# Sort steps dealt into the first feed-forward part, the pivot search behind it in bfloat16 products, and key block gathers beside the first attention

## The chip, the cores and the metric

The program runs on one core of one Trainium2 chip. The metric is device microseconds from start to end of one launch. A core has five engines with an instruction stream each: PE (TensorE, matrix products), DVE (VectorE), ACT (ScalarE), POOL (GpSimd) and SP (SyncE), which only issues transfers here. They wait for one another by semaphores. On-chip memory has 128 partitions.

## The reference

A small language model tower over 64 sequences of 256 tokens (16,384 tokens of 64 numbers), every stage added to the running value `h`:

```
h = tok(x)                                  # embedding, two small products, layer norm
h = h + recurrence(norm(h))                 # delta-rule recurrence along each sequence
h = h + moe(norm(norm(h)))                  # 8 experts 64->128->64, gates of the top 2
h = h + window_attention(norm(h))           # windows of 64 tokens, 8 heads of 8
h = h + gat_moe(norm(h))                    # graph attention over 262,144 edges sets gates of 4 experts
```

The last stage is what needs the sort. For every token (node) it wants a softmax over the edges that end there:

```
a_src, a_dst = (g*att_src).sum(-1), (g*att_dst).sum(-1)     # g = norm(h) @ W_gat, 16 numbers per node
e   = leaky_relu(a_src[src] + a_dst[dst])
agg = segment_sum(g[src] * exp(e - segment_max(e, dst)) / denom, dst)
```

## The kernel before, in words

**Stages.** The 16,384 tokens are 128 tiles of 128 (`NT=128`), cut into two parts of 64 tiles (`PARTS`). Each part goes through the recurrence (8 iterations of 8 tiles, `it(i)`, two lanes side by side), the first feed-forward part (FFN: norm, norm again, gates, then 8 groups `k`, each of four quarters `q` for pairs of experts), window attention (16 iterations of 4 tiles) and the node stage of the graph attention (8 iterations), which writes 24 numbers per node into the `node_table` in DRAM. Part 1 starts when part 0 has ended.

**Edges.** Beside part 0 DVE sorts the 262,144 edges by destination. A key holds destination and source; 128 rows hold 2048 keys each in two buffers `K[0]`, `K[1]`. The sort is a bitonic network of 192 steps (`network()`): exchanges ("x": a minimum and a maximum over all keys, lines L1037 and L1038, or L1042 and L1043 for the first ones), "sign" (L1058) and 14 "move" steps. In a move DVE only raises `s_sd` (L1061); SP stores the block to DRAM and loads it back with rows and columns exchanged (L281, L283), and the next exchange waits for that. A 193rd step reads the 32 pivots of each row (L1065) and lets SP store the sorted keys (L285 on).

**Where the sort steps stand.** DVE's program is written out in one order. `burst(i,t,most)` places up to `most` steps at six places of a recurrence iteration, where a clock of the planner (105 us per iteration, 2.5 us per step, 22 us per move) says that the data is back. What is left after the eighth iteration follows in one piece (`while at[0]<SORT`).

**Search.** For each of 32,768 node boundaries the kernel looks for the position in the sorted keys. *Pivots*: 32 chunks; DVE writes a 0/1 matrix `stp` (L1163, two buffers), PE multiplies it by the pivots' steps `dpv` (8 products of 128x128 by 128x32, float32), and DVE counts (`pivots_counted`, L1152 to L1154). The result `idx2` (L1168) frees POOL, which gathers 256 times 128 blocks of 64 keys (L420), 32 gathers in each of 8 rounds, into two landing buffers. *Rounds*: DVE compares a landed round with the thresholds (`search_round`, L1047 on); round r's gathers wait until round r-2 is used. In the kernel before the pivots stand between the recurrence and the FFN, and the rounds at fixed places: one before the gates, one behind them, one in front of each FFN group from k=3 on, one behind the FFN. `keys_apart` (L1185) splits the keys into source and destination and stands between the FFN's first two norms.

**POOL behind it.** When part 0's rows of the node table are stored (`s_tst`, L425), POOL gathers the table's rows for the early edges (960 gathers, L433), scatters the nodes' own terms (256, L442; the second half waits for part 1's node stage), gathers the rows of the late edges (1088, L450) and last the sums at the ends of the segments (256, L460). DVE works on what lands.

All products go through the one helper on L464 (`mm`), so a tile's name and shape tell them apart. L1289 is the FFN's multiplication by the gates, L1294 its sum, L1275 the addition to `h_res`; L1320 to L1332 are attention; L1174 to L1179 the norm.

## Time and profile before

| | |
|---|---|
| median of 3 runs | 5481.16 us (5477.91 to 5487.49) |
| the profiled execution, its own time | 5501.64 us |
| its span (first to last instruction) | 5499.9 us |
| busy: PE / DVE / ACT / POOL | 2728.7 / 2414.3 / 1248.0 / 2915.7 us |
| mean granted TensorE clock | 0.678 of 2.4 GHz |
| packets | 345,120, of which 214,943 under 512 bytes |

The page gives 1.7 us between the span and the profiled execution's own time. The profiled execution took 20.5 us more than the median; durations come from it. No engine is busy more than 53% of the span, so shares of busy time don't tell what bounds the kernel; the chain of waits and the order of the stages do. The granted clock of TensorE has two levels, 1.2 and 2.4 GHz; a clock of 0.50 in a stretch is the lower level throughout, 1.00 the upper.

### The profile page before, as it was taken

The page shows a single profiled execution, that of the slowest core. Times are in us where ns is not written, and L with a number is a line of the kernel's source. Part 1 is how long each engine was busy: PE and PEld are TensorE (multiplying, and loading weights), DVE is VectorE, ACT ScalarE, POOL GpSimd, SP SyncE. Part 2 cuts the span into 40 slices and gives each one's busy share as a digit, 9 for nine tenths or more (in the row PEclk, how much of TensorE's full clock was granted, in tenths as well). Part 3 has the DMA queues.
Part 4 walks back from the last instruction along what each step waited for, and adds up shares of the span by engine and source line. Part 5 has one row for each costly group of instructions (what it writes and reads, how often), then busy time and mean ns, then how long its engine had stood idle before and what let it go on. Part 6 is the DMA issues. An engine that isn't in the chain of part 4 may idle for free.

```text
span 5499.9 us, 73623 instructions
## 1 busy us (share of the span) xinstructions
PE 2728.7 (50%) x28112; PEld 2055.3 (37%) x29104; DVE 2414.3 (44%) x5221; ACT 1248.0 (23%) x2738; POOL 2915.7 (53%) x2870
## 2 busy tenths in 40 slices
PE   4667676258468767777587872022423324241000
PEld 3555565253157656565434662011212212121000
DVE  8855556555366523333446760023232323232234
ACT  2223222014244433333344540000110101010000
POOL 0000000037710077777767777777777777776774
PEclk8788877558679788888798985555555555555555
DMA  2024332305200091111162111021212222121113
GB/s 71 5 40 51 47 41 36 55 10 119 55 3 0 19 22 27 25 27 30 16 124 35 21 21 32 3 66 42 57 45 53 57 42 62 36 51 43 40 40 81
DMA packets 345120, 226.72 MB, mean 41 GB/s; under 512 B 214943, under 2 KB 302848, under 8 KB 342336
## 3 DMA queue, kind: packets, MB, share of 16 engines
q1 hardware_dynamic: 247472, 164.51, 15.2%
q0 software_dynamic: 92464, 49.28, 7.3%
q10 hardware_dynamic: 4896, 8.92, 0.7%
q8 instruction: 203, 3.33, 0.3%
q14 instruction: 85, 0.70, 0.0%
HBM read 136.08 MB, written 86.40 MB: 40 GB/s over the span
## 4 chain that ended last, share of the span: by engine, by line
POOL 52%; issue 18%; DVE 13%; PE 12%; DMA 3%; ACT 2%; POOLq 0%; SPq 0%; DVEq 0%; ACTq 0%
POOL arena L450 21%; POOL arena L433 17%; PE bank L464 12%; POOL arena L460 5%; POOL edge_dst_terms L442 4%; POOL arena L420 4%; DVE arena L1038 2%; DVE arena L1037 2%; DVE arena L1043 1%; DMA early_rows<-arena 1%; DVE arena L1042 1%; DVE arena L1320 1%; DVE arena L1325 1%; DMA arena<-sort_exchange 1%; DMA xT_d<-arena 0%
## 5 line engine op out<-in xcount | busy, mean ns | idle before, releaser
L464 PE MATMUL bank<-arena 64*64 64x64 f32 (+11 forms) x25478 | 2322.0, 296 | 1852.0 <-ACT arena L938 1200.1
L464 PEld LDWEIGHTS bank<-arena 64*64 64x64 f32 (+5 forms) x25478 | 1578.7, 166 | 1908.1 <-issue 1625.8
L450 POOL DMA_INDIRECT arena<-node_table,arena x1088 | 1157.4, 1064 | 331.6 <-issue 331.6
L433 POOL DMA_INDIRECT arena<-node_table,arena x960 | 939.3, 978 | 347.4 <-issue 288.3
L413 POOL IOTA arena<- 128x1024 int32 x1 | 1.0, 988 | 940.6 <-DVE h_res L1131 940.6
L420 POOL DMA_INDIRECT arena<-sorted_keys,key_block_idx x256 | 277.0, 1082 | 304.8 <-DVE key_block_idx L1168 227.1
L464 PE MATMUL bank<-ident,arena 128*128 128x128 f32 (+2 forms) x2048 | 304.8, 325 | 227.3 <-ACT arena L908 80.3
L464 PEld LDWEIGHTS bank<-ident,arena 128*128 128x128 f32 (+2 forms) x2048 | 273.4, 196 | 261.4 <-DVE arena L1326 106.6
L1380 DVE COPY arena<-arena 128x4 f32<-128x4 f32 x32 | 5.9, 184 | 807.2 <-DMA arena<-node_table,arena 806.7
L940 ACT ACTIVATE arena<-arena 128x512 f32<-128x512 f32 x32 | 20.1, 629 | 1408.0 <-DVE arena L1388 1408.0
L183 PEld LDWEIGHTS <-zero_b 128*128 128x128 bf16 x992 | 97.7, 99 | 581.3 <-DVE arena L1103 118.7
L460 POOL DMA_INDIRECT arena<-sums_sorted,arena x256 | 261.7, 1022 | 79.1 <-issue 77.7
L442 POOL DMA_INDIRECT edge_dst_terms<-arena x256 | 258.9, 1011 | 83.5 <-issue 83.5
L425 POOL TENSOR_TENSOR pool_spare<-pool_spare 1x1 f32<-1x1 f32 x2 | 0.6, 286 | 401.6 <-DMA node_table<-arena 401.6
L893 ACT ACTIVATE arena<-bank,arena 128x512 f32<-128x512 f32 x256 | 161.9, 684 | 225.7 <-PE bank L464 224.8
L1395 DVE TENSOR_TENSOR_SCAN arena<-arena 128x64 f32<-128x64 f32 x640 | 186.4, 372 | 1.1
L464 PE MATMUL bank<-pivot_steps,arena 128*128 128x32 f32 x512 | 109.4, 401 | 116.9 <-DVE arena L1163 116.9
L1037 DVE TENSOR_TENSOR arena<-arena 128x1024 f32<-128x1024 f32 x116 | 141.9, 1224 | 39.1 <-DMA arena<-sort_exchange 36.0
L1289 DVE SCALAR_TENSOR_TENSOR arena<-bank,arena 128x512 f32<-128x512 f32 x128 | 89.8, 746 | 154.9 <-PE bank L464 109.1
L464 PEld LDWEIGHTS bank<-pivot_steps,arena 128*128 128x128 f32 x512 | 109.3, 333 | 117.1 <-issue 117.1
L1364 DVE TENSOR_TENSOR arena<-bank,arena 128x512 f32<-128x512 f32 x64 | 44.3, 692 | 223.1 <-PE bank L464 223.1
L1038 DVE TENSOR_TENSOR arena<-arena 128x1024 f32<-128x1024 f32 x116 | 141.4, 1219 | 0.0
(377 smaller groups left out, 3046.4 us busy)
## 6 DMA issues: line engine op xcount, KB each, us to landing
arena<-expert_gates SPq DMA_DIRECT2D x64, 512.0 KB, 7.4
arena<-node_table,arena POOLq DMA_INDIRECT x2048
sums_sorted<-arena SPq DMA_DIRECT2D x32, 768.0 KB, 3.3
expert_out<-arena SPq DMA_DIRECT2D x64, 256.0 KB, 2.6
arena<-expert_out SPq DMA_DIRECT2D x16, 1024.0 KB, 5.8
sort_exchange<-arena SPq DMA_DIRECT2D x14, 1024.0 KB, 3.9
early_rows<-arena POOLq DMA_DIRECT2D x15, 768.0 KB, 3.6
arena<-early_rows SPq DMA_DIRECT2D x15, 768.0 KB, 4.3
```

Source lines behind the costliest of these rows:

```text
L183: if me=="pe": nc.tensor.ldweights(zero_b[:,:],tile_position=(0,0))
L420: G.indirect_dma_start(out=rows[:,u,:],out_offset=None,in_=keysb,in_offset=bass.IndirectOffsetOnAxis(ap=idx2[:,t:t+1],axis=0)).then_inc(s_ ...
L433: G.indirect_dma_start(out=early_b[j%2][:,c,:],out_offset=None,in_=tbl, in_offset=bass.IndirectOffsetOnAxis(ap=gidx[:,j*CW+c:j*CW+c+1],axi ...
L442: G.indirect_dma_start(out=ad_e,out_offset=bass.IndirectOffsetOnAxis(ap=sidx[:,h*NT+t:h*NT+t+1],axis=0), in_=nodeG[:,t,20:24],in_offset=No ...
L450: G.indirect_dma_start(out=rch[:,j%NB,c,:],out_offset=None,in_=tbl, in_offset=bass.IndirectOffsetOnAxis(ap=gidx[:,CA+j*CW+c:CA+j*CW+c+1],a ...
L460: G.indirect_dma_start(out=at[:,t,:],out_offset=None,in_=sums_d,in_offset=bass.IndirectOffsetOnAxis(ap=eidx[:,h*NT+t:h*NT+t+1],axis=0)).th ...
L464: mm=lambda o,a,b,st=True,sp_=True: nc.tensor.matmul(o,a,b,start=st,stop=sp_,skip_group_check=True)
L893: A.activation(B.hT[:,n%2,:],B.ps[n%2][:,:],ACT.Gelu,bias=fb1[:,n%8:n%8+1]).then_inc(B.ge,1)
L1037: V.tensor_tensor(y[:,:,0,:],x[:,:,0,:],x[:,:,1,:],ALU.min)
L1038: lk(V.tensor_tensor(y[:,:,1,:],x[:,:,0,:],x[:,:,1,:],ALU.max))
L1289: V.scalar_tensor_tensor(out=B.tm[:,q%2,:] if q else B.acc[:,k%2,:],in0=B.ps[2+m%2][:,:],scalar=fb2[l][:,q:q+1],in1=B.G[:,k%2,q,:],op0=ALU ...
L1395: last=V.tensor_tensor_scan(R[:,:,f],xe[:,0,:,head(f)],R[:,:,f],cin[:,f:f+1],ALU.mult,ALU.add)
```

## The change

1. **Sort plan.** A function `sort_plan()` makes, before the program is built, lists of how many steps stand at each place: seven places in a recurrence iteration (`PLACES`, with 9, 2, 5, 3, 4, 1 and 1 as the most), two before the gates of the first FFN part (`PRE_AT`), and one behind each of the 32 quarters of it (`FFN_AT`, two at most). What is left (`LEFT`) stands behind the FFN. SP's moves are dealt in the same way.
2. **Pivots.** They stand behind the FFN of part 0 instead of in front of it, and the steps `dpv` are split into a high and a low part in bfloat16; `stp` is bfloat16 too. Each float32 product becomes two bfloat16 ones.
3. **Rounds.** `keys_apart` stands behind the norm that precedes attention; rounds stand in front of attention's iterations 4, 6, 9, 11, 13 and 15, and the last two behind attention.

How many steps stand at each place (x exchange, s sign, M move; a slash between places):

| recurrence iteration | before (6 places) | after (7 places) |
|---|---|---|
| 0 and 1 | 12/3/5/4/5/3 | 9/2/5/3/4/1/1 |
| 2 | 4/0/2/0/5/3 | 9/2/5/2/0/1/1 |
| 3 | 5/0/3/0/0/3 | 0/2/5/3/3/0/1 |
| 4 | 10/0/0/4/0/3 | 2/2/5/3/3/0/1 |
| 5 | 10/0/0/4/1/3 | 3/0/5/3/4/1/0 |
| 6 | 10/0/0/4/2/0 | 0/2/3/0/0/1/1 |
| 7 | 12/1/0/4/3/0 | 9/2/0/0/4/1/1 |
| sum | 160 | 140 |

Then before: 33 steps in one piece. After: xxx before the gates; in the FFN's groups (four quarters each) xx/xx/xx/xx, sM/-/-/xx, xx/xx/M/-, -/xx/xx/xx, xx/xx/xs/M, -/-/xx/xx, xx/xM/-/-, xx/xx/xx/xx; behind it xxxM.

```diff
+PLACES=((2.0,9),(29.0,2),(40.0,5),(53.0,3),(64.0,4),(80.0,1),(92.0,1))
+BEFORE_FFN=2
+def sort_plan():
+    net=[kind for kind,d,up in network()]+["move"]
+    at=0; ready=0.0
+    def take(now,most):
+        nonlocal at,ready
+        n=m=0
+        while n<most and at<len(net) and now>=ready:
+            now+=2.4; n+=1
+            if net[at]=="move": ready=now+20.0; m+=1
+            at+=1
+        return n,m
+    rec=[[take(i*100.0+t,most) for t,most in PLACES] for i in range(ITA)]
+    t=ITA*100.0+10.0
+    pre=[take(t+30.0*k,3) for k in range(BEFORE_FFN)]
+    t+=30.0*BEFORE_FFN
+    ffn=[[take(t+36.0*k+9.0*q,2) for q in range(4)] for k in range(ITA)]
+    left=len(net)-at
+    return rec,pre,ffn,left
...
-        axs=bump(AX0,W0); stp=[axs([1024]),axs([1024])]; iov=axs([1024],I32); cnt=axs([16,31])
+        axs=bump(AX0,W0); stp=[axs([1024],BF16),axs([1024],BF16)]; iov=axs([1024],I32); cnt=axs([16,31])
...
                         for h,s in HALVES:
                             sp.dma_start(B.G[s,k%2,:,:],gd[...]...).then_inc(B.gl[k%2],16)
+                    if part==0 and k: sort_moves(sum(m for _,m in FFN_AT[k-1]))
+                if part==0:
+                    sort_moves(2*XL+1-moved[0])
+                    sp.dma_start(keys2,K[0]).then_inc(s_ks,16)
+                    sp.dma_start(pvp[1:P,:],pv[0:P-1,:]).then_inc(s_ks,16)
...
                 for B in FL: pe.wait_ge(B.ha,k1); pe.wait_ge(B.ge,8*k1)
-                if part==0: pe.wait_ge(s_w2,16*8)
+                if part==0:
+                    for c in range(32):
+                        b=c//2
+                        pe.wait_ge(s_sp,c+1)
+                        if c%2==0 and b>=8: pe.wait_ge(s_sq,b-7)
+                        for u in range(8):
+                            k=8*(c%2)+u
+                            mm(PS[b%8][:,k*32:(k+1)*32],stp[c%2][:,u*P:(u+1)*P],dph[:,:],True,False)
+                            r=mm(PS[b%8][:,k*32:(k+1)*32],stp[c%2][:,u*P:(u+1)*P],dpl[:,:],False,True)
+                        r.then_inc(s_sm,1)
+                    pe.wait_ge(s_sq,16)
+                    pe.wait_ge(s_w2,16*8)
...
-                if run==0:
-                    while at[0]<SORT: sort_step()
...
                 norm(part,H,xn)
-                if part==0: keys_apart()
+                if part==0: steps_of(PRE_AT[0])
                 norm(part,xn,xn,s_xn)
-                if part==0: search_round()
+                if part==0: steps_of(PRE_AT[1])
...
-                if part==0: search_round()
...
-                    if part==0 and k>=3: search_round()
                     for q in range(4):
...
+                        if part==0: steps_of(FFN_AT[k][q])
                 for l in range(2): result(l,k1-1)
...
+                if part==0:
+                    steps_of((LEFT,0))
+                    pivots()
                 norm(part,H,xn)
-                if part==0: search_round()
+                if part==0: keys_apart()
...
-                    if part==0 and i==9 and used[0]<8: search_round()
+                    if part==0 and i in (4,6,9,11,13,15): search_round()
```

DVE, the end of part 0's recurrence (its last write to `h_res`) and what follows. Before:

```order
L1131 TENSOR_TENSOR h_res<-bank,arena 128x256 x2
L1037 TENSOR_TENSOR arena<-arena 128x1024
L1038 TENSOR_TENSOR arena<-arena 128x1024
L1037 TENSOR_TENSOR arena<-arena 128x2x512
L1038 TENSOR_TENSOR arena<-arena 128x2x512
```

and after, where L1157 is the same write and L1178 on the norm:

```order
L1157 TENSOR_TENSOR h_res<-bank,arena 128x256 x2
L1169 MEMSET eps 128x1
L1171 CAST iota8<-iota8_i 128x8
L1172 TENSOR_SCALAR iota_below_four<-iota8 128x4
L1264 MEMSET arena 128x1056
L1265 TENSOR_SCALAR arena<-iota8 128x8
L1178 TENSOR_REDUCE ln_stat<-h_res 128x32
```

The 33 sort steps and the pivot search no longer stand between the recurrence and the norm.

DVE, the first quarters of the FFN's group 0. Before (L1289 the gates' multiplication, L1294 the sum):

```order
L1289 SCALAR_TENSOR_TENSOR arena<-bank,arena 128x512 x4
L1294 TENSOR_TENSOR arena<-arena 128x512 x2
L1289 SCALAR_TENSOR_TENSOR arena<-bank,arena 128x512 x2
L1294 TENSOR_TENSOR arena<-arena 128x512 x2
L1289 SCALAR_TENSOR_TENSOR arena<-bank,arena 128x512 x2
L1294 TENSOR_TENSOR arena<-arena 128x512 x2
```

and after, where L1317 and L1322 are the same two and L1069, L1070 a sort exchange:

```order
L1317 SCALAR_TENSOR_TENSOR arena<-bank,arena 128x512 x2
L1069 TENSOR_TENSOR arena<-arena 128x8x128
L1070 TENSOR_TENSOR arena<-arena 128x8x128
L1069 TENSOR_TENSOR arena<-arena 128x16x64
L1070 TENSOR_TENSOR arena<-arena 128x16x64
L1317 SCALAR_TENSOR_TENSOR arena<-bank,arena 128x512 x2
L1322 TENSOR_TENSOR arena<-arena 128x512 x2
L1069 TENSOR_TENSOR arena<-arena 128x32x32
L1070 TENSOR_TENSOR arena<-arena 128x32x32
```

Two exchanges now stand between one quarter's work and the next.

SP, from the FFN's first gate loads (L334) on, after the change; L307 and L309 are a sort move's store and load:

```order
L334 DMA arena<-expert_gates 64x4x512 x12
L307 DMA sort_exchange<-arena 128x2048
L309 DMA arena<-sort_exchange 128x128x16
L334 DMA arena<-expert_gates 64x4x512 x4
L307 DMA sort_exchange<-arena 128x2048
L309 DMA arena<-sort_exchange 128x128x16
L334 DMA arena<-expert_gates 64x4x512 x8
```

Before, the 32 gate loads stood in one row with no move between them.

## Rows read from the trace of the kernel before

**Rows 1.** Page, part 4: the chain that ended last, shares of the span.

```profile
POOL 52%; issue 18%; DVE 13%; PE 12%; DMA 3%; ACT 2%; POOLq 0%; SPq 0%; DVEq 0%; ACTq 0%
POOL arena L450 21%; POOL arena L433 17%; PE bank L464 12%; POOL arena L460 5%; POOL edge_dst_terms L442 4%; POOL arena L420 4%; DVE arena L1038 2%; DVE arena L1037 2%; DVE arena L1043 1%; DMA early_rows<-arena 1%; DVE arena L1042 1%; DVE arena L1320 1%; DVE arena L1325 1%; DMA arena<-sort_exchange 1%; DMA xT_d<-arena 0%
```

**Rows 2.** POOL's waits: us in total, times, longest us.

```profile
POOL pool_spare L425 <- DMA node_table<-arena: 401.6, 2, 401.0
POOL arena L420 <- DVE key_block_idx L1168: 227.1, 1, 227.1
POOL edge_dst_terms L442 <- issue: 83.5, 256, 3.0
```

**Rows 3.** Stretches: length; busy us of PE, PEld, DVE, ACT, POOL; clock; DMA; GB/s.

```profile
36.00:948.00 912.00, 604.52 (x8896) 508.18 (x9392) 600.24 (x1069) 248.79 (x576) 0.00 (x0) 0.78 0.26 34
948.00:1055.00 107.00, 0.00 (x0) 0.00 (x0) 70.02 (x62) 0.00 (x0) 0.99 (x1) 0.51 0.33 39
1055.00:1176.00 121.00, 109.41 (x512) 109.30 (x512) 50.36 (x121) 0.00 (x0) 0.00 (x0) 0.50 0.09 29
1285.00:1508.00 223.00, 151.47 (x600) 51.22 (x600) 103.96 (x148) 73.44 (x116) 173.03 (x165) 0.80 0.46 94
1508.00:1845.00 337.00, 259.59 (x3072) 214.11 (x3072) 228.11 (x549) 153.34 (x458) 18.39 (x16) 0.86 0.01 2
```

**Rows 4.** DVE's timeline, one iteration of part 1's recurrence, which holds no sort step.

```profile
2128.75 0.48 DVE L1086 TENSOR_SCALAR arena<-arena 128x512 f32<-128x512 int32 x1
...
2145.55 0.43 DVE L1089 TENSOR_SCALAR arena<-arena 128x512 f32<-128x512 f32 x1 [15.13 <-ACT arena L825]
...
2155.16 0.83 DVE L1096 TENSOR_TENSOR arena<-arena 128x256 f32<-128x256 f32 x2 [3.16 <-ACT arena L834]
...
2168.89 0.69 DVE L1106 TENSOR_TENSOR arena<-bank,arena 128x512 f32<-128x512 f32 x1 [7.57 <-PE bank L464]
...
2192.62 0.69 DVE L1114 TENSOR_TENSOR arena<-bank,arena 128x512 f32<-128x512 f32 x1 [7.92 <-PE bank L464]
...
2220.87 0.48 DVE L1086 TENSOR_SCALAR arena<-arena 128x512 f32<-128x512 int32 x1
```

**Rows 5.** DVE's timeline, a sort move's return and the exchange behind it.

```profile
993.57 1.23 DVE L1037 TENSOR_TENSOR arena<-arena 128x1024 f32<-128x1024 f32 x1 [18.00 <-DMA arena<-sort_exchange]
...
995.97 1.22 DVE L1037 TENSOR_TENSOR arena<-arena 128x1024 f32<-128x1024 f32 x1
```

**Rows 6.** A bfloat16 weight load (zeros, in the recurrence): ns min/median/max.

```profile
L183 PEld LDWEIGHTS <-zero_b x992: 95/96/151, 36.9 to 2680.1; 128*128 128x128 bf16 x199
```

**Rows 7.** DVE's timeline, the pivot search; a chunk that waits, and a count.

```profile
1061.27 0.06 DVE L1156 MEMSET pivot_steps<- 128x1 f32 x1 [5.15 <-DMA pivot_nodes_row_above<-pivot_nodes]
...
1085.03 0.75 DVE L1163 TENSOR_SCALAR arena<-arena,shifted_firsts 128x1024 f32<-128x1024 int32 x1 [2.66 <-PE bank L464]
1085.70 0.67 DVE L1152 TENSOR_TENSOR arena<-bank,arena 128x496 f32<-128x496 f32 x1
...
1087.11 0.17 DVE L1154 SCALAR_TENSOR_TENSOR search_a<-bank,search_b 128x16 f32<-128x16 f32 x1
```

**Rows 8.** DVE's timeline, FFN of part 0: quarters, and a round that waits.

```profile
1309.46 1.41 DVE L1289 SCALAR_TENSOR_TENSOR arena<-bank,arena 128x512 f32<-128x512 f32 x2 [2.73 <-PE bank L464]
...
1323.80 1.41 DVE L1289 SCALAR_TENSOR_TENSOR arena<-bank,arena 128x512 f32<-128x512 f32 x2 [1.53 <-PE bank L464]
1327.94 1.41 DVE L1289 SCALAR_TENSOR_TENSOR arena<-bank,arena 128x512 f32<-128x512 f32 x2 [2.73 <-PE bank L464]
...
1441.92 2.29 DVE L1047 TENSOR_TENSOR arena<-arena,node_thresholds 128x2048 f32<-128x2048 f32 x1 [22.26 <-DMA arena<-sorted_keys,key_block_idx]
...
1447.06 2.73 DVE L1289 SCALAR_TENSOR_TENSOR arena<-bank,arena 128x512 f32<-128x512 f32 x4
```

**Rows 9.** DVE's timeline, the start of attention's second iteration.

```profile
1568.60 2.48 DVE L1320 TENSOR_TENSOR arena<-bank,arena 128x512 f32<-128x512 f32 x4 [1.89 <-ACT arena L906]
```

**Rows 10.** POOL alone in part 1's attention: length, POOL busy, clock, DMA share, GB/s.

```profile
2970.00:3200.00 230.00, 168.07 (x178) 0.95 0.13 20
```

More of the change, by code:

```diff
@@ L276, in _, with sort_moves @@
             sp.dma_start(tbl.rearrange("(p a b) f -> p a (b f)",p=P,a=8),zfill[:,0:384].unsqueeze(1).broadcast_to((P,8,384))).then_inc(s_zs,16)
[L277 to L279 removed]
+            moved=[0]
+            def sort_moves(count):
+                for _ in range(count):
+                    moved[0]+=1; n=moved[0]
                     sp.wait_ge(s_sd,n)
[L281 to L294 removed]
+                    if n<=2*XL:
+                        k=merge_at((n+1)//2,(n+1)%2)
+                        sp.dma_start(sort2,K[k]).then_inc(s_st,16)
+                        sp.wait_ge(s_st,16*n)
+                        sp.dma_start(K[1-k].rearrange("p (q l) -> p q l",l=16),sortx).then_inc(s_sl,16)
+            sort_moves(sum(m for row in REC_AT for _,m in row))
             for l in range(LANES):
@@ L309, in _ @@
                 k0,k1=t0//8,t1//8; b0,b1=k0//2,k1//2
+                if part==0: sort_moves(sum(m for _,m in PRE_AT))
                 sp.wait_ge(s_ws,b1)
@@ L1067, in sort_step, with steps_of, burst @@
                     V.tensor_copy(rowbase[:,:],rowp_f[:,:]).then_inc(s_sd,1)
-            SORT=len(NET)+1
-            clock=[0.0]
-            def burst(i,t,most):
-                now=i*ITER_US+t
-                while most and at[0]<SORT and now>=hold[0]:
-                    kind=NET[at[0]][0] if at[0]<len(NET) else "move" if at[0]==len(NET) else "x"
-                    sort_step(); most-=1; now+=2.5
-                    if kind=="move": hold[0]=now+ROUND_US
-            ITER_US=105.0; ROUND_US=22.0
+            def steps_of(place):
+                for _ in range(place[0]): sort_step()
             dve.wait_ge(s_key,1)
             def it(i):
+                def burst(k):
+                    if i<ITA: steps_of(REC_AT[i][k])
                 def step(fn,*need):
```

97 lines of the change are left out of this document (43 added, 54 removed).

## The prediction

> **What bounds the kernel now.** I read the chain of waits first: POOL holds 52% of it, and its gathers on L433, L450 and L460 with the scatters on L442 make 47% of the span [rows 1]. Then POOL's waits, to see what starts that work: it waited once for a long time, 401.0 us, for the last store of part 0's node table (L425), and behind that the longest wait of any scatter was 3.0 us [rows 2]. So from the moment at which part 0's table is stored (call it S, 1933 in the profiled execution's time) POOL runs without a pause, and part 1's compute is hidden beside it. What comes before S decides, microsecond for microsecond. Then the stretches [rows 3] tell what stands before S: the recurrence 912 us (36 to 948); 107 us in which PE and ACT do nothing and DVE finishes the sort; 121 us of pivot search; then the norms and gates (109 us to the FFN's first multiplication at 1285), the FFN with 223 us, norm and attention with 337, and the last 88 to S. Nothing in the change touches a later instruction. I therefore work out the shift of S and take it as the shift of the end.
>
> **The recurrence, from 912 to about 846.** An iteration without sort steps takes 92.1 us (2128.75 to 2220.87), and in it DVE waits 15.1 us behind the first place, 3.2 behind the second, 7.6 behind the third, 7.9 behind the fifth [rows 4]. An exchange takes 2.40 us, measured start to start [rows 5]. Steps are free up to the wait that follows them; the rest lengthens the iteration. Twelve steps at the first place cost 12 x 2.4 - 15.1 = 13.7, nine cost 6.5. At the second place three cost 4.0 and two 1.6; at the third five cost 12 - 9 = 3 in both kernels (the wait of 7.6 and some shorter ones behind it). For the fourth and fifth I take 2.9 and 5.7 us as covered, less than the longest single wait: four steps on the fourth cost 6.7, three 4.3; five on the fifth 6.3, four 3.9. Three on the old last place cost about 3.8, one on each of the two new ones nothing. With the numbers of steps in the table of the change this gives, iteration by iteration, 37.5, 37.5, 10.1, 3.8, 13.6, 16.0, 12.2, 20.4 before: 151 us over 8 x 92.1 = 737, together 888, where the trace has 912. The missing 24 us I can't place. After: 19.3, 19.3, 11.1, 8.9, 8.9, 10.1, 1.6, 10.4, together 90, so 827 without the missing part and 841 to 851 with it. I take 846: -66 us (bounds: -56, all of the 24 stays and places three to five hide less; -80).
>
> **The sort's tail and the pivots in front of the norm: -107 and -121** [rows 3]. Both go. The norms start at once. SP's loads of the FFN's weights, which lay beside the pivots, now lie beside the two norms; they are needed only at the first turned tile. Between the gates and the first multiplication one search round goes that was hidden in a wait for the gate loads; in front of the gates go one round (5.1, as 1441.92 to 1447.06 in [rows 8]) and the splitting of the keys (2.6), and three exchanges come (7.2). Together 0.
>
> **The FFN, from 223 to about 238: +15.** Before, a group of four quarters takes 18.5 us (1309.46 to 1327.94), a quarter 4.14, and three rounds then make DVE wait some 21 us each for POOL's gathers (22.26 in the row shown) [rows 8]; DVE is busy 104 of 223 us [rows 3]. Those waits go. The steps come: 40 exchanges of 2.4 and 2 signs of 1.3 make 99 us. DVE's own work is 104 less five rounds of 5.1 = 78, so DVE alone has 177. A quarter with two exchanges takes 2.6 + 4.8 = 7.4 on DVE, more than PE's 4.14, and PE works one quarter ahead, in the other bank: I count it as hidden. Eleven quarters have no exchange and are bound by PE: some 1.5 us each, 16. The start with its wait for the gate loads: 5. And the four moves: a landing takes 18.0 us [rows 5] when the DMA engines are free; here the gate loads share them (share 0.46 on the mean, with half of the time empty [rows 3]), so I take 18 to 26. Between a move and the next exchange the plan leaves two to four quarters, worth some 8 to 14 us at PE's pace where the plan's own clock counts 9 each, so each move makes DVE wait 5 to 15 us: four times 10 is 40. The sum is 238. Bounds: 210 (landings hidden) and 290 (below).
>
> **The pivots behind the FFN: +73.** The last four steps (7.4), the wait for the rows stored by SP (5.2, as [rows 7]), the split of the steps and the 32 shifts (3.6), the chunks, and 1 us for the index. A chunk has 16 products as before, when 512 took 109.4 us at the lower clock, 1.2 GHz (0.50 throughout) [rows 3]: 3.42 us per chunk, 0.214 per product, and DVE waited 2.66 us in each [rows 7]. A bfloat16 load of 128 columns takes 96 ns in the median, alone [rows 6]. The trace has no bfloat16 product of this shape. Bounds: PE as slow as now, 109 us; PE no longer the bound, DVE's own work of 0.67 per chunk and 1.5 per two chunks [rows 7], 1.42 x 32 = 46 us. The nearest row is the load: 16 x 0.107 (half of 0.214, a little above 96 ns) = 1.7 us, 55 us in all. I take 56.
> The Trainium skill (TensorE: Matmul & The Clock Gate, Weight-path perf modes) says that weights of 128 columns that aren't float32 load by a faster path, measured at about twice the speed. By that, PE falls below DVE's pace, the chunks take 46 us, and the total is 10 us less. The row of zero weights shows 96 ns, which doesn't look like the fast path, so I stay with 56.
>
> **Attention, from 337 to 398: +61.** From the index (T) on POOL gathers eight rounds. In the FFN's stretch POOL issued 165 gathers in 223 us, 1.35 us each [rows 3], so 43.3 us per round; beside part 1's attention 178 in 230 us, 1.29 each [rows 10]: attention doesn't slow them. Norm (26.5), splitting the keys (2.6), constants and the first products (8): attention starts at T+37 and takes 18.7 us per iteration (1545 to 1845, 16 of them). A round costs DVE 5.1 us, of which the 1.9 us wait at an iteration's start hides a part [rows 9]: 3.3 to 5.1 each. Round 0 is used at iteration 4 (T+112 to 117), so round 2's gathers can't start before T+117 and land at T+162; from there they follow each other at 43 us, held up once for 12 by round 2's use at iteration 9: round 6 at T+348, round 7 at T+392. Attention ends at T+356. DVE then waits some 30 us for round 7, uses it (5.1), and starts the next norm at T+398. Before it started 337 us after the FFN. The last 88 us to S are unchanged. Bounds: +45 (gathers at 1.29), +80.
> The Trainium skill (SBUF — State Buffer, Who interferes with whom) warns that GpSimd's own access is shut out while VectorE runs an instruction with two on-chip inputs or in a two-port mode. Attention's instructions read a bank and one tile; only the round's own comparison has two, 2.3 us per round. By that rule the cost is 2 us per round at most; it carries the slow rival below.
>
> **The sum.** -66 - 107 - 121 + 0 + 15 + 73 + 61 = -145. The profiled execution of 5501.6 would become 5356.6; the median lies 20.5 lower, 5336.
>
> **Rivals.**
> *The steps don't hide in the FFN.* Then a quarter with two exchanges costs 4.14 + 4.8 = 8.9: 8 x 18.5 + 99 + 40 + 5 = 292, and S moves by -91: 5390. For it: a PE that waits drops to the lower clock, as in the stretch with the three waits, where the mean was 0.80 [rows 3]; at half the clock a quarter needs 8.3 us of PE. Against: two banks.
> *It hides better.* The missing 24 us of the recurrence go, landings are covered, the chunks take 46 us, gathers 1.29: -14 -20 -10 -12: 5336 - 56 = 5280 at the extreme; 5308 when half comes true. For it: the waits of rows 4 that I didn't count.
> *Slower: POOL starves beside attention.* Rounds 2 to 7 stand in one chain, six gathers of 32, between T+117 and the next norm. If DVE's dense work shut out POOL's descriptors, a round of 43 us would become 80: 6 x 37 = 222 us more, 5336 + 222 = 5558. It decides from 67 us per round (145/6 = 24 more). Against it stand the 1.29 us beside part 1's attention.
> *The chain doesn't follow S.* Something else ends late (part 1's node stage before its scatters, a transfer), and half of the gain or more goes: 5410 to 5480. Against it: the 3.0 us of rows 2, and everything in part 1 moves with S.
>
> **How the numbers follow.** My forecast 50%, the first rival 20%, the second 17%, the slow one 3%, the last 6%, of which a third ends within 0.2% of no change or above; 4% for a stall that I didn't see, half of it slower. The time is the forecast's, 5336. Its own range is 5315 to 5365. The range for 8 in 10 takes in most of both neighbours: 5296 to 5400. This kernel's runs differ by 0.17%, so no change means within 0.2%, 11 us. Faster 0.94, within 0.02, slower 0.04.
>
> **What would show it.** The last write to h_res of the first recurrence near 882; the norm directly behind it; the FFN's first multiplication near 990 and its end near 1230; DVE waits of 5 to 15 us for the exchange's landing in it, four times; 512 bfloat16 products in 50 to 60 us at the lower clock; POOL's gathers (L420's) from about 1303 on, 43 us a round; one wait for a landing behind attention of 20 to 35 us; POOL's first table gather near 1790 and all behind it unchanged. Wrong: a group of the FFN near 36 us, rounds over 50 us, a POOL wait in the scatters, or a recurrence above 870.

## The result and the profile after

Changed kernel: median 5319.76 us of 4 runs (5313.64 to 5343.19). Kernel before: 5484.32 us of 4 runs (5477.91 to 5487.49). Ratio 0.9713, 95% interval 0.9688 to 0.9738: faster, by 164.6 us. The profiled execution took 5313.64 us with a span of 5311.9; it is the fastest of the four, and the profiled one of the kernel before (5501.64) lies above all four of its timed runs. Measured again later, beside other kernels, the changed kernel gave 5323.54 us and 0.971 (0.9688 to 0.9732).

Line numbers moved: the search gathers L420 are L450 now, the table gathers L433 are L463, the scatters L442 are L472, the wait for part 0's table L425 is L455. POOL's waits of the changed kernel, as in [rows 2] (total, times, longest):

```profile
POOL arena L450 <- DVE key_block_idx L1212: 395.1, 1, 395.1
POOL pool_spare L455 <- DMA node_table<-arena: 92.3, 2, 90.2
POOL edge_dst_terms L472 <- issue: 83.6, 256, 3.0
```

POOL's long wait for the table is 90.2 us instead of 401.0: the search gathers moved into it. They were finished 90 us before the table was stored, so no table gather waited for them; only the last search round made DVE wait, by 19.65 us (below). Behind the table nothing changed: the longest wait of a scatter is 3.0 us again.

The stretches of the changed kernel, to be read against [rows 3]:

```profile
core 0: us, PE busy (x) PEld busy (x) DVE busy (x) ACT busy (x) POOL busy (x), PEclk, DMA share, GB/s
36.00:875.00 839.00, 586.14 (x8896) 492.66 (x9392) 556.00 (x1031) 248.05 (x576) 0.00 (x0) 0.81 0.22 31
875.00:981.00 106.00, 43.17 (x328) 31.74 (x328) 60.33 (x70) 37.57 (x47) 0.99 (x1) 0.60 0.28 38
981.00:1208.00 227.00, 161.22 (x600) 54.54 (x600) 174.89 (x214) 73.44 (x116) 0.00 (x0) 0.82 0.68 105
1208.00:1225.00 17.00, 0.00 (x0) 0.00 (x0) 10.64 (x49) 0.00 (x0) 0.00 (x0) 0.50 0.20 70
1225.00:1271.00 46.00, 19.44 (x512) 16.14 (x512) 44.65 (x84) 0.00 (x0) 0.00 (x0) 0.50 0.06 22
1308.00:1625.00 317.00, 261.64 (x3045) 207.25 (x3041) 231.42 (x535) 141.04 (x440) 206.06 (x214) 0.90 0.09 22
1625.00:1656.00 31.00, 0.07 (x1) 0.00 (x0) 10.70 (x12) 0.00 (x0) 18.32 (x19) 0.52 0.08 20
```

They are: the recurrence; norms, gates and the wait for the gates' loads; the feed-forward part (FFN); the sort's last steps and the set-up of the pivot search; its 32 chunks; attention; the wait for the last search round. (Between 1271 and 1308 lie the norm and attention's first products, between 1656 and 1742 what stores the table.) POOL's first table gather starts at 1742.08 instead of 1933. The part behind it is 3569.8 us long, 2.9 more than before. So the end did follow S, and S moved by -191 where I had said -145:

| stage | before | predicted | after |
|---|---|---|---|
| recurrence | 912 | 846 | 839 |
| sort's tail, search ahead of the norm | 107 + 121 | 0 | 0 |
| norms, gates, to the first multiplication | 109 | 109 | 106 |
| FFN | 223 | 238 | 227 |
| behind the FFN, to the index (T) | 0 | 73 | 64 |
| norm and attention, to the next norm | 337 | 398 | 385 |
| from there to S | 88 | 88 | 86 |

### The profile page after: what moved, and what is told of

Its sections match the earlier page's. It is cut to its first block, busy times and chain, and to the rows that moved or that the text cites. A ratio compares the mean times of both kernels' runs of the same rounds, so it can differ in the third digit from the quotient of the medians.

```text
span 5311.9 us, 73647 instructions
## 1 busy us (share of the span) xinstructions
PE 2631.8 (50%) x28112; PEld 1943.7 (37%) x29104; DVE 2408.9 (45%) x5226; ACT 1245.7 (23%) x2738; POOL 2893.2 (54%) x2870
## 4 chain that ended last, share of the span: by engine, by line
POOL 51%; issue 19%; DVE 14%; PE 9%; DMA 4%; ACT 1%; SPq 0%; POOLq 0%; DVEq 0%; ACTq 0%
POOL arena L480 22%; POOL arena L463 18%; PE bank L494 9%; POOL arena L490 5%; POOL edge_dst_terms L472 5%; POOL arena L450 2%; DVE arena L1070 2%; DVE arena L1069 2%; DMA arena<-sort_exchange 1%; DMA early_rows<-arena 1%; DVE arena L1075 1%; DVE arena L1074 1%; DMA sort_exchange<-arena 0%; DVE arena L1207 0%; DVE arena L1179 0%
## 5 line engine op out<-in xcount | busy, mean ns | idle before, releaser
L463 POOL DMA_INDIRECT arena<-node_table,arena x960 | 939.5, 979 | 350.0 <-issue 288.3
L450 POOL DMA_INDIRECT arena<-sorted_keys,key_block_idx x256 | 253.5, 990 | 518.8 <-DVE key_block_idx L1212 395.1
L494 PE MATMUL bank<-ident,arena 128*128 128x128 f32 (+2 forms) x2048 | 293.1, 316 | 255.9 <-ACT arena L950 94.4
L972 ACT ACTIVATE arena<-arena 128x512 f32<-128x512 f32 x32 | 20.1, 629 | 1410.8 <-DVE arena L1420 1410.8
L472 POOL DMA_INDIRECT edge_dst_terms<-arena x256 | 258.4, 1009 | 83.6 <-issue 83.6
L925 ACT ACTIVATE arena<-bank,arena 128x512 f32<-128x512 f32 x256 | 161.9, 684 | 219.1 <-PE bank L494 219.1
L1069 DVE TENSOR_TENSOR arena<-arena 128x1024 f32<-128x1024 f32 x116 | 141.7, 1221 | 35.9 <-DMA arena<-sort_exchange 33.2
L1317 DVE SCALAR_TENSOR_TENSOR arena<-bank,arena 128x512 f32<-128x512 f32 x128 | 90.2, 746 | 139.8 <-PE bank L494 79.9
L1070 DVE TENSOR_TENSOR arena<-arena 128x1024 f32<-128x1024 f32 x116 | 141.2, 1217 | 0.0
L970 ACT ACTIVATE arena<-bank,arena 128x512 f32<-128x512 f32 x128 | 82.7, 688 | 177.2 <-PE bank L494 177.0
L940 ACT ACTIVATE arena<-arena 128x512 f32<-128x512 f32 x128 | 77.5, 630 | 192.1 <-DVE arena L1358 192.1
```

Source lines behind the costliest of these rows:

```text
L450: G.indirect_dma_start(out=rows[:,u,:],out_offset=None,in_=keysb,in_offset=bass.IndirectOffsetOnAxis(ap=idx2[:,t:t+1],axis=0)).then_inc(s_ ...
L463: G.indirect_dma_start(out=early_b[j%2][:,c,:],out_offset=None,in_=tbl, in_offset=bass.IndirectOffsetOnAxis(ap=gidx[:,j*CW+c:j*CW+c+1],axi ...
L472: G.indirect_dma_start(out=ad_e,out_offset=bass.IndirectOffsetOnAxis(ap=sidx[:,h*NT+t:h*NT+t+1],axis=0), in_=nodeG[:,t,20:24],in_offset=No ...
L494: mm=lambda o,a,b,st=True,sp_=True: nc.tensor.matmul(o,a,b,start=st,stop=sp_,skip_group_check=True)
L925: A.activation(B.hT[:,n%2,:],B.ps[n%2][:,:],ACT.Gelu,bias=fb1[:,n%8:n%8+1]).then_inc(B.ge,1)
L1069: V.tensor_tensor(y[:,:,0,:],x[:,:,0,:],x[:,:,1,:],ALU.min)
```

## The experiments

The experiments ran on three chips, so I compare ratios to the kernel before, measured on the same chip, and stages of the profiled executions from their own starts. The intervals of two ratios leave a difference of 15 to 27 us open; where less than 30 us is at stake, the reading rests on the stages.

**Float32 products.** The flags, the tile of steps and the product go back to float32; the search stays where the change put it.

```diff
-mm(PS[b%8][..],stp[c%2][..],dph[:,:],True,False)
-r=mm(PS[b%8][..],stp[c%2][..],dpl[:,:],False,True)
+r=mm(PS[b%8][..],stp[c%2][..],dpv[:,:])
```

> The changed kernel with the pivot search's products in float32 again (256 products of one set of steps instead of 512 of two halves, the compared flags in float32); the search stays behind the feed-forward part. Theory: TensorE's pace bounds the loop again, 3.42 us per chunk as before the change, 109 us in all instead of 46, so S (the store of part 0's node table and the start of POOL's table gathers) moves from 1742 to about 1805 and the time by +63, to about 5383. Rival: the products hide behind DVE's 1.41 us per chunk also in float32, because the engine is free of other work there: no change. Second rival: the time behind S gives part of it back, +30.

Measured: 5376.81 us, ratio 0.9822 (0.978 to 0.9864), by the ratios 60 us above the changed kernel (some 27 either way); S 66.6 us later in the trace, of which 2 lie in its recurrence. The search's stretch in it:

```profile
1228.00:1340.00 112.00, 109.41 (x512) 109.30 (x512) 46.95 (x83) 0.00 (x0) 0.00 (x0) 0.50 0.02 6
```

TensorE is busy in all of it, as before the change; the theory holds and both rivals fall. The bfloat16 halves are worth some 60 us by themselves.

**The same edit in the kernel before.** Only the halves, with the search ahead of the norm as it was.

```diff
-r=mm(PS[b%8][..],stp[c%2][..],dpv[:,:])
+mm(PS[b%8][..],stp[c%2][..],dph[:,:],True,False)
+r=mm(PS[b%8][..],stp[c%2][..],dpl[:,:],False,True)
```

> The kernel before with only the pivot search's products changed to two bfloat16 halves; the search stays between the sort's tail and the norms. Theory: DVE bounds the chunks at 1.41 us there too, at the same lower clock: the search's 121 us become 59 (46 for the chunks, 1.4 more for the halves), S and the end 62 us earlier, the ratio to the kernel before 0.9887. Rival: behind the sort's tail TensorE has stood still for 107 us and is slower than behind the feed-forward part; chunks of 1.7 us, 55 in all: 0.990 to 0.991. Second rival: SP's loads of the feed-forward part's weights were hidden beside the search, and the norms or the first turned tile now wait for them: 0.993 or more.

Measured: 5414.98 us against 5473.32, ratio 0.9885 (0.9858 to 0.9912). From the recurrence's end to the index 162 us instead of 228. The place of the search makes no difference to its pace, and no wait appeared behind it. So of the 165 us, about 60 come from the number format, as both experiments say; the other 105 are what is left for the order of the work.

**Each product six times.**

```diff
+for _ in range(5): mm(PS[b%8][..],stp[c%2][..],dph[:,:],True,True)
+for _ in range(5): mm(PS[b%8][..],stp[c%2][..],dpl[:,:],True,True)
```

> The changed kernel with every bfloat16 product of the pivot search issued six times (3072 instead of 512; the result is the same, since only the last pair is kept). Theory: a product with its load of 128 columns starts 27 ns behind the one before it at the lower clock, as the starts in the trace of the changed kernel say; 96 products take 2.6 us per chunk, more than DVE's 1.41, and with the hand-over the 32 chunks take about 90 us instead of 46: S and the end +44. Rival, the duration of the load's row (96 to 105 ns) is its pace, and the starts in the trace are modelled: 96 x 0.1 = 9.6 us per chunk, 307 us in all: +260.

Measured: one run, 5368.78 us; from the FFN's end to the index 108.9 us instead of 63.6, +45. The groups of the search's stretch (busy and mean of one, then idle time before them):

```profile
L494 PE MATMUL bank<-pivot_steps_high,arena 128*128 128x32 bf16 x1536 | 79.0, 177 | 22.8 <-DVE arena L1209 20.2 <-issue 2.3
L494 PEld LDWEIGHTS bank<-pivot_steps_low,arena 128*128 128x128 bf16 x1536 | 63.9, 96 | 3.9 <-issue 3.9
L1209 DVE TENSOR_SCALAR arena<-arena,shifted_firsts 128x1024 bf16<-128x1024 int32 x32 | 24.0, 753 | 40.5 <-PE bank L494 40.0
```

Now DVE waits for TensorE, 40 us. 3072 products in 91 us are 30 ns each with the hand-over between chunks, while the mean of a load is 96 and that of a product 177 ns. Duration is not pace: a load is on its way for 96 ns, and the next starts some 27 ns behind it. The first chunk was at the lower clock (0.50 from 1233 to 1236), a later one at 2.4 GHz (1.00 from 1260 to 1290):

```profile
1234.03 0.29 PE L494 MATMUL bank<-pivot_steps_high,arena 128*128 128x32 bf16 x5 [20.17 <-DVE arena L1209]
1234.16 0.29 PE L494 MATMUL bank<-pivot_steps_low,arena 128*128 128x32 bf16 x5
1234.30 0.19 PE L494 MATMUL bank<-pivot_steps_high,arena 128*128 128x32 bf16 x1
...
1262.11 0.28 PE L494 MATMUL bank<-pivot_steps_high,arena 128*128 128x32 bf16 x5
1262.23 0.28 PE L494 MATMUL bank<-pivot_steps_low,arena 128*128 128x32 bf16 x5
1262.36 0.18 PE L494 MATMUL bank<-pivot_steps_high,arena 128*128 128x32 bf16 x1
```

Ten products start in 0.27 us at the one and in 0.25 at the other. DVE, which waits for the first chunk, goes on at 1236.79, 2.76 us behind its first product: 29 ns for each of the 96 at the lower clock.

**No step in the FFN.** All 42 steps and four transfers that stood there go behind it.

```diff
-ffn=[[take(t+36.0*k+9.0*q,2) for q in range(4)] for k in range(ITA)]
+ffn=[[(0,0)]*4 for k in range(ITA)]
```

> The changed kernel with no sort step in the feed-forward part: the 42 steps and four exchanges between partitions that it held stand behind it, in front of the pivot search, with the four that stood there already. Theory: what they cost in the feed-forward part is only what DVE's own work leaves open. Without them the part is bound by TensorE (8 times 18.5 us and the start): 155 us instead of 227; behind it 44 exchanges of 2.4, two signs of 1.3 and four landings of 20 us, 188 in place of 7.4: S and the end +109 us, about 5425. Rival: the steps don't hide and only stand there in a row: the part falls by the steps' whole 99 us and the landings' 28, to 100 us, and the time rises only by the landings' 52. Second rival: the part stays over 200 us, because the gates' loads bound it: +180.

Measured: 5409.07 us, ratio 0.9873 (0.9844 to 0.9902), 88 us above the changed kernel by the ratios.

```profile
993.00:1143.00 150.00, 141.01 (x600) 45.09 (x600) 79.32 (x127) 73.46 (x116) 0.00 (x0) 0.96 0.50 103
1143.00:1324.00 181.00, 0.15 (x2) 0.01 (x1) 105.69 (x96) 0.00 (x0) 0.00 (x0) 0.50 0.40 47
```

The FFN alone is 150 us, bound by TensorE at a granted clock of 0.96; with the steps it is 227 at 0.82. The steps and landings that cost 171 us behind it (235 less 64) cost 77 inside. About half of them hides.
Both rivals fall. The size is off: 94 us (171 less 77) where I expected 109 (181 less 72).

**An exchange between partitions with almost no data.** 16 partitions in whole rows of 8 KB (128 KB, not 64 as the expectation says) instead of 1 MB read back in pieces of 64 B.

```diff
-sp.dma_start(sort2,K[k]).then_inc(s_st,16)
+sp.dma_start(sort2[0:16],K[k][0:16]).then_inc(s_st,16)
-sp.dma_start(K[1-k].rearrange("p (q l) -> p q l",l=16),sortx).then_inc(s_sl,16)
+sp.dma_start(K[1-k][0:16],sort2[0:16]).then_inc(s_sl,16)
```

> The changed kernel with the sort's exchanges between partitions cut down to 16 partitions (64 KB, in rows of 4 KB, both ways) instead of 128 in pieces of 64 B; the keys are then not sorted, the node numbers gathered later lie in part 0's half of the table, and the count that lets the table gathers start is a constant, so only the stages up to S are read. Theory: TensorE's stalls in the recurrence with no releaser (4.90, 2.25, 9.09 and 7.67 us, four of them, 23.9 in all) come from its instructions being loaded behind the exchange's 1 MB in small packets. They go, with the 5.6 us of waits for landings: the recurrence 812 instead of 839 us. In the feed-forward part the four waits of 7 us go: 199 instead of 227. S about 1685. Rival: the stalls belong to the places in the program (branches, loading at a loop's end) and stay: recurrence 833. Second rival: the four waits in the feed-forward part only move to TensorE's pace: 215 to 220.

This kernel leaves out most of the exchange, so its keys are not sorted and only its stages are read. It is about the 24 us of the recurrence that my sum of the kernel before did not explain. In the changed kernel the seventh iteration has only six exchanges and still takes 107.4 us. TensorE there (start, us, in brackets what it waited for):

```profile
717.80 5.01 PE L494 MATMUL bank<-arena 64*64 64x64 f32 x121
730.49 1.75 PE L494 MATMUL bank<-arena 64*64 64x64 f32 x23 [7.67 <-issue]
```

It stopped for 7.67 us with its data ready. The DMA view of these microseconds (tenths of share; then queues):

```profile
DMA  9999999999999999999999999900000000000000
...
q1 hardware_dynamic: 1831, 0.46, 88.2%
q8 instruction: 1, 0.02, 1.3%
```

The DMA engines were full with the exchange's small packets (q1), and one packet of instructions (q8) was among them. They fell empty at about 727.5, and TensorE went on 3 us later, at 730.49. (In the kernel before, at 578.0 and 580.98.) The changed kernel's recurrence has four such stops (4.90, 2.25, 9.09, 7.67 us). Three of them stand at the same places in all ten executions of this recurrence (4.5 to 4.9, 9.0 to 9.3 and 5.4 to 8.0 us), so they are no accident of one. The one of 9.09 stands at an iteration's start, where 2.3 to 2.6 us are idle in the same way without an exchange, so some 21 of the 24 us go with the exchange. The kernel before has five, 21.1 us in all, the first one of these:

```profile
351.21 3.02 PE L464 MATMUL bank<-arena 64*64 64x64 f32 x41 [6.81 <-issue]
452.41 3.88 PE L464 MATMUL bank<-arena 64*64 64x64 f32 x57 [2.11 <-issue]
```

With tiny exchanges the stretches (recurrence, FFN) are:

```profile
36.00:845.00 809.00, 574.00 (x8896) 482.37 (x9392) 556.66 (x1033) 247.62 (x576) 0.00 (x0) 0.83 0.04 10
951.00:1150.00 199.00, 159.55 (x600) 52.77 (x600) 174.46 (x214) 73.35 (x116) 0.00 (x0) 0.84 0.40 83
```

809 and 199 us, as expected to 3 us (812 and 199); the seventh iteration takes 91.5 us, and the stops over 2.6 us are gone; what is left are the six at iterations' starts. S came only at 1729 and not at 1685, since the search gathers, whose indices are others here, took longer (a DVE wait of 47 us behind attention). Shown is that the exchange's traffic stops TensorE. Whether its volume or its small pieces do it is open, since the edit cut both. That it does so by holding up its instructions is what the q8 packet suggests; nothing here shows it apart.

**Search rounds earlier.**

```diff
-if part==0 and i in (4,6,9,11,13,15): search_round()
+if part==0 and i in (1,3,5,7,9,11,13,15): search_round()
```

> The changed kernel with the eight search rounds at attention's iterations 1, 3, 5, 7, 9, 11, 13 and 15 instead of 4, 6, 9, 11, 13, 15 and two behind it. Theory: attention's end is set by POOL's chain of gathers, 40.3 us per round, which stood still 28.4 and 18.25 us because a round's buffer was not yet used. With the uses a round earlier it never stands still, the last landing wait (19.65 us) goes, and two rounds of 5.1 us lie in attention (about 5.9 us each there): from the index to the next norm 364 instead of 385 us, S and the end 20 us earlier, about 5300. Rival: DVE waits in attention's first iterations for rounds that have not landed (each earlier use costs what the gathers are late), so the same or slower, 5315 to 5330.

In the changed kernel POOL stood still twice, because round 0's and round 2's buffers were not yet used, and DVE waited at the end:

```profile
1385.60 0.95 POOL L450 DMA_INDIRECT arena<-sorted_keys,key_block_idx  x1 [28.40 <-DVE arena L1226]
1484.47 0.94 POOL L450 DMA_INDIRECT arena<-sorted_keys,key_block_idx  x1 [18.25 <-DVE arena L1226]
1650.45 2.29 DVE L1079 TENSOR_TENSOR arena<-arena,node_thresholds 128x2048 f32<-128x2048 f32 x1 [19.65 <-DMA arena<-sorted_keys,key_block_idx]
```

Measured: 5288.45 us, ratio 0.9661 (0.9622 to 0.97). None of these three waits is left, and from the index to the next norm it takes 365 us instead of 385 (364 expected). The rival falls. The ratios say 28 us with some 25 either way, the stage 20.

**Exchanges in the wait for the gates.** Nine exchanges directly ahead of the FFN, a landing counted as 14 us in it.

```diff
-pre=[take(t+30.0*k,3) for k in range(BEFORE_FFN)]
+pre=[(0,0)]*BEFORE_FFN
+post=take(t,9)
...
+if part==0: steps_of(POST)
```

> The changed kernel with nine exchanges between the gates and the feed-forward part's first multiplication, where DVE waits 23.8 us for the gates' loads; three of them come from in front of the gates and six from the feed-forward part, whose steps are dealt anew with landings counted as 14 us; six steps instead of four are left behind it. Theory: exchanges in that wait are free. From the first norm to the first multiplication 98 to 100 us instead of 106 (7.2 us of exchanges gone in front of the gates), the feed-forward part and the steps left 215 instead of 235 us; S and the end 25 us earlier, about 5295. Rival: the wait is set by DVE's order and grows with the exchanges (each of the nine costs 2.4 us), then the first part gives 0 and the sum is -7 or less. Second rival: landings in the feed-forward part, closer to each other now, take back what was won.

The first multiplication of the changed kernel and of this one:

```profile
981.09 0.75 DVE L1317 SCALAR_TENSOR_TENSOR arena<-bank,arena 128x512 f32<-128x512 f32 x1 [23.80 <-DMA arena<-expert_gates]
```

```profile
980.69 0.75 DVE L1327 SCALAR_TENSOR_TENSOR arena<-bank,arena 128x512 f32<-128x512 f32 x1 [2.40 <-DMA arena<-expert_gates]
```

Measured: 5300.89 us, ratio 0.9686 (0.9646 to 0.9726). Nine exchanges lie in the wait for nothing, and from the first multiplication to the index it takes 272 us instead of 290. But the first multiplication did not come earlier: the three exchanges that had stood ahead of the gates were free there too. DVE now waits at that place for TensorE's turning of the tiles:

```profile
938.89 0.49 DVE L1293 TENSOR_TENSOR arena<-bank,arena 128x128 f32<-128x128 f32 x2 [7.93 <-PE bank L503]
```

So -18 instead of -25, by the stages; the ratios of the two kernels (0.9686 and 0.9713) don't tell them apart.

**All waits filled, up to three steps per quarter.** Against the kernel of the experiment before:

```diff
-pre[1]=(0,0)
-post=take(t,9)
+pre[1]=take(t-30.0,3)
+post=take(t,8)
-t+=24.0; hold[0]=14.0
+t+=24.0; hold[0]=16.0
-n,m=take(t,2)
+n,m=take(t,3)
...
+if part==0 and i in (1,3,5,7,9,11,13,15): search_round()
```

> The changed kernel with both edits that the runs before showed to pay, and one more: search rounds at attention's iterations 1, 3, ... 15; the three exchanges in front of the gates stay (they lie in a wait of 7.9 us for TensorE's turning); eight exchanges lie in the 23.8 us wait for the gates' loads; the rest is dealt in the feed-forward part up to three per quarter, with a landing counted as 16 us, and none is left behind it. Theory: each filled wait is worth its own length: -20 us from the rounds, -18 from the exchanges behind the gates, and 7 to 9 more from the three in front of the gates and the landings that are waited for less: S 46 us earlier than in the changed kernel, near 1697, and the time near 5272. Rival: three exchanges in one quarter (9.8 us) let TensorE's clock fall, and the feed-forward part gets as long as it was: 5290. Second rival: the gains overlap, because both shift POOL's chain: 5280.

Measured: 5302.52 us, ratio 0.968 (0.9656 to 0.9704), no better than the earlier rounds alone. From the first multiplication to the index 292 us, although all of the sort was in it. Twice DVE stood like this:

```profile
1074.51 0.75 DVE L1327 SCALAR_TENSOR_TENSOR arena<-bank,arena 128x512 f32<-128x512 f32 x1 [9.80 <-issue]
1081.36 0.75 DVE L1327 SCALAR_TENSOR_TENSOR arena<-bank,arena 128x512 f32<-128x512 f32 x1 [6.11 <-DMA arena<-expert_gates]
```

The forecast of 5272 was wrong, and my first rival's cause (the clock) too: the granted clock in the FFN was 0.81, as in the changed kernel (0.82). Two of the next three experiments look for the cause.

**Only the two edits that paid, and a deal by hand; the changed kernel beside them.** The second combines both edits with at most two steps per quarter, the third writes the FFN's deal out.

```diff
+FFN_COUNTS=((1,0,0,0),(0,2,2,2),(1,0,0,0),(0,2,2,2),(2,2,2,1),(0,0,0,0),(2,2,2,2),(0,0,0,0))
```

> The changed kernel itself, once more, beside the next two on the same chip. Theory: the recurrence takes 839 to 853 us in different executions of the same code (as in the traces so far), so the median lies between 5314 and 5330 and the ratio to the kernel before between 0.970 and 0.973.

> The changed kernel with exactly the two edits that paid alone: search rounds at attention's iterations 1, 3, ... 15, and nine exchanges between the gates and the feed-forward part with at most two per quarter behind them (six left behind the part). Theory: they lie in different stages and add: -20 and -18, S 38 us earlier than in the changed kernel on the same chip, ratio to it 0.993. From the first multiplication to the index 272 us, from the index to the next norm 365. Rival: they overlap as in the run with all waits filled, where the feed-forward part was longer: then the part itself is over 225 us here too.

> As the run before, with three exchanges kept in front of the gates, eight and a sign behind them, and the feed-forward part's steps dealt by hand: at most two per quarter, each transfer between partitions followed by four quarters without a step, eleven exchanges left behind the part. Theory: the longer feed-forward part of the run with all waits filled came from three steps per quarter and from gate loads that stood behind a transfer (two waits of 16 us), not from filling the waits. Here neither occurs: from the first multiplication to the index 265 us (7 less than with nine exchanges moved), S 45 us earlier than in the changed kernel. Rival: the gates' loads are late here too, because the transfers come at the start of a row: 285 us, and no gain over the run before.

Measured on one chip: the changed kernel 5323.54 us (0.971, 0.9688 to 0.9732); both edits 5283.35 us (0.964, 0.9616 to 0.9665); by hand 5292.78 us (0.9653, 0.9626 to 0.9679). The two edits add up, 40 us below the changed kernel, and the rival falls: the FFN took 205 us. From the first multiplication to the index it takes 274 us instead of 290, from there to the next norm 368 instead of 385; these 33 us are the edits', and 6 more lie in the recurrence, whose code is the same. It has the lowest time of all, but its interval overlaps those of the rounds alone and of the deal by hand. By hand the FFN itself is shorter (193 us instead of 205), but from the first multiplication to the index it takes 280 us and not 265: eleven exchanges are left behind it, and the gates' loads are late here too. SP's queue in that kernel, around the transfer in the fifth row:

```profile
1113.64 0.33 SPq L317 DMA_DIRECT2D sort_exchange<-arena  x1
1118.21 0.72 SPq L319 DMA_DIRECT2D arena<-sort_exchange  x1
1118.97 20.25 SPq L344 DMA_DIRECT2D arena<-expert_gates  x8
```

The gates' loads were issued 0.8 us behind the exchange's reading back, and landed in 16.0 us in the median (7.6 over the whole of the changed kernel, 9.5 for its eight loads behind the FFN's third exchange). DVE then waited 9.00 us with no releaser and 4.43 for the gates:

```profile
1138.10 0.75 DVE L1328 SCALAR_TENSOR_TENSOR arena<-bank,arena 128x512 f32<-128x512 f32 x1 [9.00 <-issue]
1143.28 0.75 DVE L1328 SCALAR_TENSOR_TENSOR arena<-bank,arena 128x512 f32<-128x512 f32 x1 [4.43 <-DMA arena<-expert_gates]
```

The pair of waits is the same as in the experiment with all waits filled. The rival that names the loads holds in this: the gates came late and nothing was gained over both edits. But an exchange ahead of the loads is not enough. In the changed kernel SP's queue reads the same:

```profile
1124.57 0.72 SPq L309 DMA_DIRECT2D arena<-sort_exchange  x1
1125.33 23.97 SPq L334 DMA_DIRECT2D arena<-expert_gates  x8
```

The first of these loads landed in 16.1 us, and DVE waited for no gates: the row that needs them started at 1150.90, 25.6 us behind their issue. In the deal by hand the row in between has no step, DVE was done with it at 1129.1, 10 us behind the issue, and stood until 1138.10.

## Why the prediction came out

The median was forecast as 5336 and was 5319.76, within the forecast's own range (5315 to 5365), and the main mechanism is as written: S moved, and the end with it. Step by step:

- *Recurrence, 846 forecast.* The trace has 839. The same code gave 839 to 853 in the ten profiled executions of the changed kernel and of kernels with its recurrence, 846 on the mean. The bound of 841 was too narrow by what executions differ. The 24 us that I could not place are, by the tiny exchanges, mostly TensorE's stops during a transfer: 21.1 us in the trace of before, which I didn't search for idle time without a releaser. After the change 24 us of stops are there too, so keeping them in the sum was right for a reason I didn't know. That the sum met the mean is partly luck: with tiny exchanges the same steps took 809 us (one execution) where my sum without the remainder says 827, so the steps were costed too high, by up to 18 us, and a wait of 5.6 us for a landing stood in no term. (In the last iteration of the kernel before I had also counted a sign as an exchange: 19.3 us there and not 20.4.)
- *Sort's tail, pivots ahead of the norm.* Gone, as said. Between norm and gates 0 was said and -3 came; the three exchanges there are hidden.
- *FFN, 238 forecast, 227.* DVE is busy 175 us (177 said). A quarter with two exchanges takes 7.31 us to the hundredth in three that follow each other, so the steps bound DVE and nothing else does. The failing term is the landings, 4 x 10: they cost 7.0, 6.7, 7.0 and 7.0, since a landing took 18.1 to 20.0 us from the mark to the exchange. The gates' loads hardly slowed it, and I had allowed up to 26.
- *Pivots behind the FFN, 73 forecast, 64.* The failing term is the chunks, 56 where 46 came. DVE walks at its own pace and never waits:

```profile
1230.93 1.41 DVE L1207 TENSOR_SCALAR arena<-arena,shifted_firsts 128x1024 bf16<-128x1024 int32 x2
1233.74 1.41 DVE L1207 TENSOR_SCALAR arena<-arena,shifted_firsts 128x1024 bf16<-128x1024 int32 x2
1236.56 1.41 DVE L1207 TENSOR_SCALAR arena<-arena,shifted_firsts 128x1024 bf16<-128x1024 int32 x2
```

  I had read the load's duration, 96 ns [rows 6], as the time until the next one can start. The trace of before held the warning: there a float32 load lasts 333 ns on the mean, and one came every 0.214 us (109.4 us for 512). A duration that is longer than the pace says nothing of the pace. The sixfold products give 30 ns where I had set 107.
  By the rule of the Trainium skill that I had put aside (TensorE: Matmul & The Clock Gate, Weight-path perf modes), weights of 128 columns that aren't float32 take a faster path, and DVE's 46 us would bound. The trace agrees, with 46; that it is this path which makes the loads fast, no run here shows apart.
- *Attention, 398 forecast, 385.* The round of gathers took 40.3 us and not 43.3: I had taken the gathers' pace from the FFN's stretch, the slower of two rows. Six rounds in a chain make 18 us; the second stop of POOL was 18 and not 12. The wait for round 7 was 19.65 us where some 30 were said. Why that row was slower, the traces show too. In the FFN of the kernel before 26 of 164 gathers lasted over 1.1 us instead of 0.94, 17 us more in all, and each of the 26 ran beside a DVE instruction that reads two on-chip tiles (L1294 or L1047). In the changed kernel's attention it is 5 of 230, each beside a round's comparison:

```profile
1420.64 2.28 DVE L1079 TENSOR_TENSOR arena<-arena,node_thresholds 128x2048 f32<-128x2048 f32 x1
```

```profile
1421.84 1.90 POOL L450 DMA_INDIRECT arena<-sorted_keys,key_block_idx  x1 [0.30 <-issue]
```

  The gather ended 0.82 us behind DVE's instruction, as did the other four. So POOL was held up, by 1.0 to 1.4 us each time, within the 2 us per round that the prediction allowed.
- *The start from the profiled execution.* My -145 against it, -188 in the trace, -165 in the medians. The profiled execution of before had a slow attention: iterations of 18.9 us at a granted clock of 0.91, next to one of 17.2 at 1.00:

```profile
1587.20:1606.10 18.90, 16.38 (x201) 13.62 (x198) 12.56 (x33) 8.99 (x29) 0.00 (x0) 0.91 0.00 0
1662.30:1679.50 17.20, 14.68 (x198) 11.92 (x196) 12.52 (x33) 8.86 (x29) 0.00 (x0) 1.00 0.00 0
```

  In the kernel before with the halves alone, whose attention has the same work, the 300 us are 283 at 0.96. The changed kernel's attention waits for POOL at its end, so what its clock does hardly counts. Some 17 us of the trace's difference are therefore the execution's, not the change's, and the changed kernel's profiled recurrence is 7 us shorter than its mean; the rest are the terms above, all costed too high. That the median was missed by only 16 us owes something to two errors of opposite sign (costs too high, and a start that a typical execution doesn't have).

Of the rivals, *hides better* had the direction: landings, chunks and gathers, three of its four, came true at -12, -10 and -13. *The steps don't hide* falls with 227 us. *POOL starves* falls with 40.3 us per round. *The chain doesn't follow S* falls with 3569.8 us behind S.

## What to carry to other kernels

Read an engine's pace from start to start in a full row of instructions; the mean of one is latency as soon as it exceeds that. When a sum misses tens of microseconds, look for idle time without a releaser and for what the DMA engines did in it, before the remainder is carried along. Work dealt into waits is worth their length only while nothing that the next stage needs comes late by it: where loads stand behind a transfer on its queue, leave more time than their longer landing (here 16 us) before they are needed. Use a double buffer as soon as it has landed.

## What the runs showed of the hardware that I had not expected

- A bfloat16 product of 128x128 weights with 32 columns, its load included, took 25 to 30 ns, at either clock; the float32 one 427 ns at the lower clock (109.4 us for 256 products, each in two records).
- Beside a transfer of 1 MB in pieces of 64 B TensorE stopped, with its data ready, for up to 7.67 us (9.09 at an iteration's start); with 128 KB in long rows no stop over 2.6 us was left.
- An indirect gather on POOL took 0.94 us. In the FFN of the kernel before, the 29 gathers that began while DVE ran L1294 or L1047 (two on-chip tiles as inputs) took 1.08 to 3.04 us and ended 0.2 or 0.8 us behind that instruction (one 1.4); the 17 that were under way when it began took 0.94 or 0.95. Beside attention's instructions on a bank and a tile it stayed at 0.94.
- The same instructions of the recurrence took 839 to 853 us in ten executions; the mean granted clock was 0.81 in the shortest and 0.79 in the longest.
